# Applying two attention terms as two accumulated matmuls instead of one matmul of their sum

## The chip, the core and the metric

The kernel runs on one core of a Trainium2 chip. The core has TensorE (PE; its weight loads are listed as PEld), VectorE (DVE), ScalarE (ACT), GpSimd (POOL) and SyncE (SP), each with its own in-order queue, joined by semaphores. The metric is device microseconds of one execution.

## What is computed

A small language-model tower over x of shape (8, 1024): token embedding, a lattice attention with 8 heads, a causal attention and a mixture of experts. Only the lattice attention matters here. Per batch and head, on 1024x1024 scores:

```python
scores = ttt_filter(q @ k.T / 8)              # scaled by 1/PHI where int(|s|*1618) % 9 is 0, 3 or 6
attn = softmax(scores)
attn = attn * (sin(C1 * attn) * exp(-attn * attn / PHI) + cos(C2 * attn))
ctx = attn @ v
out = ctx @ Wo + bo
```

## The kernel before

The program runs four stages one behind the other: embed, lattice, causal, experts. The lattice stage handles 64 heads (8 batches of 8). For a head, att holds the softmax rows with queries on the partitions, as 8 row tiles of 128x1024. To apply them to the values, whose key index must be on the partitions, TensorE transposes them: `fill` (L565 to L574) turns four 128x128 blocks into one PSUM bank of 128x512. A head has 16 such half tiles, k (or d) = 0 to 15. TensorE turns each twice:

- gauss part (L607 to L614): half tile d to a bank, ScalarE squares it (L451) and takes the exponential (L463), VectorE multiplies with the bank into ag (L508).
- sine part (L615 to L625): half tile k again to one of four banks. ScalarE takes the cosine into work (L435), VectorE multiplies bank and work into work (L476): this is the cosine term. TensorE then subtracts whole turns in the bank (L586, a matmul with -I), ScalarE takes the sine in the bank (L440), VectorE multiplies bank and ag into sinb (L482): this is the sine term. GpSimd adds the two into sinb (L377, semaphore summed). TensorE multiplies the sum, in four 128x128 blocks, with the 128x64 values vo into outp (L635, semaphore av). I call these four matmuls an AV group; there are 16 a head, and all accumulate in the bank outp.

work and sinb are rings of 8 half tiles. outp is used in turn by the projections of the next head (L560), by the values (L646) and by the AV groups; VectorE adds the finished outp to the result at L487.

The order is written out by hand. Every engine runs the same loop over 44 steps a head and at each step does what the table of numbers at L283 to L297 places there, for three heads at once: the scores of head t (L599, then magnitudes on ScalarE L458 and the filter on VectorE), the exponentials and gauss part and early sine part of head t-1, the end of the sine part of head t-2. GAUSS is step 56 of a head, SINE step 72; fill k of the sine part is at SINE + k, its L586 at SINE + k + 3, L482 at SINE + k + 4, the GpSimd sum at SINE + k + 5, and AV group k at SINE + 6 + 8k/5 (L292). At one step TensorE takes first the oldest head's work. The exponentials (L423) start at step 47 of a head, that is step 3 of the 44; the first score matmul is at step 5 and stands behind a wait for the first exponential. In the loop body two heads are written out, so that every second head has the loop's branch in it, between steps 43 and 0, in the middle of the sine part's end.

GpSimd also scales six of the eight softmax rows (L382) and does one step of the filter (L387).

Of the kernel before, what the change touches and what calls it, by code (L numbers as in the profile page):

```python
# [6 lines left out]
ALU = mybir.AluOpType  # L7
# [6 lines left out]
P = 128  # L14
B, S, D = 8, 1024, 64
# [15 lines left out]
def wait(eng, s, v):  # L31

    if not isinstance(v, int) or v > 0:
        eng.wait_ge(s, v)
# [204 lines left out]
def lattice(nc, ident, hres, xT_dram, wvo, Wq, bq, Wk, bk):  # L239
# [4 lines left out]
    RING = 8  # L244
    with ExitStack() as ctx:
# [3 lines left out]
        def sem(name):  # L249
# [9 lines left out]
        vo = sb("vo", [P, TB, D])  # L259
# [15 lines left out]
        outp = ctx.enter_context(nc.psum_tensor("outp", [P, 512], F32))  # L275

        names = ("consts loadq loadv projd qk_sb vald v_sb qk mags rounded kept factor filtered bias expd "
                 "recip weights weights2 turned xpose squared gauss agd cosd acd nned sined tmul summed av outd").split()
        (consts, loadq, loadv, projd, qk_sb, vald, v_sb, qk, mags, rounded, kept, factor, filtered, bias,
         expd, recip, weights, weights2, turned, xpose, squared, gauss, agd, cosd, acd, nned, sined, tmul, summed,  # L280
         av, outd) = (sem("l_" + n) for n in names)

        NTILE = 2 * TB  # L283
# [5 lines left out]
        EXP = STEPS + 3  # L289
        GAUSS = STEPS + 12  # L290
        SINE = STEPS + 28
        AV = [SINE + 6 + 8 * k // 5 for k in range(NTILE)]  # L292
        OUT = AV[-1] + 1
        EV = 2
        PACE = 2
# [58 lines left out]
        @block.gpsimd  # L354
        def _(pool):
            nc.gpsimd.memset(xq[D:D + 1, :], 1.0).then_inc(consts, 1)
            pool.wait_ge(consts, 1)
            nc.gpsimd.memset(xv[D:D + 1, :], 1.0).then_inc(consts, 1)
            pool.wait_ge(consts, 2)
            nc.gpsimd.memset(negI[:], 0.0).then_inc(consts, 1)  # L360
            pool.wait_ge(consts, 3)
            nc.gpsimd.affine_select(out=negI[:], in_=negI[:], compare_op=ALU.not_equal, fill=-1.0,
                                    base=0, pattern=[[-1, P]], channel_multiplier=1).then_inc(consts, 1)
            nc.gpsimd.memset(halfpi[:], math.pi / 2).then_inc(consts, 1)
            pool.wait_ge(consts, 5)
            nc.gpsimd.memset(qT[D:P], 0.0).then_inc(consts, 1)
            pool.wait_ge(consts, 6)
            nc.gpsimd.memset(kT[D:P], 0.0).then_inc(consts, 1)

            def iteration(t, par):  # L370
                for s in range(STEPS):
                    for g, p, a in stages(t, par, s):
                        k = a - SINE - 5
                        if 0 <= k < NTILE:

                            wait(pool, tmul, NTILE * g + k + 1)
                            nc.gpsimd.tensor_tensor(sinb[:, k % RING], sinb[:, k % RING], work[:, k % RING],  # L377
                                                    ALU.add).then_inc(summed, 1)
                        j = a - EXP - 1
                        if 0 <= j < TB and j not in DVE_ROWS:  # L380
                            held(pool, recip, TB * g + j + 1)
                            nc.gpsimd.tensor_scalar(att[:, p, j], att[:, p, j], rs[:, j:j + 1], TURN,  # L382
                                                    ALU.mult, ALU.mult).then_inc(weights, 1)
                        if a - FACT in SCORE:
                            n = SCORE.index(a - FACT)
                            held(pool, kept, NTILE * g + n + 1)
                            nc.gpsimd.tensor_scalar(wgt[:, n % 4], wgt[:, n % 4], 1.0, PHI,  # L387
                                                    ALU.mult, ALU.add).then_inc(factor, 1)

            over_heads(pool, iteration)  # L390

        @block.scalar
        def _(act):
# [14 lines left out]
            def iteration(t, par):  # L408
                for s in range(STEPS):
                    for c in range(2):  # L410
                        if s == PROJ + EV + 2 * c and (not isinstance(t, int) or t + 1 < NHEADS):
                            projections(t + 1, 1 - par, c)
                    for g, p, a in stages(t, par, s):
                        if a == VAL + EV:

                            wait(act, vald, g + 1)
                            wait(act, av, NTILE * g)
                            nc.scalar.activation(vo[:], outp[:].rearrange("p (t d) -> p t d", d=D),
                                                 ACT.Copy, scale=1.0 / TURN).then_inc(v_sb, 1)
                        j = a - EXP  # L420
                        if 0 <= j < TB:
                            wait(act, bias, TB * g + j + 1)
                            nc.scalar.activation(att[:, p, j], att[:, p, j], ACT.Exp,  # L423
                                                 bias=nb[:, p, j:j + 1], scale=EXPSCALE,
                                                 accum_out=ssum[:, j:j + 1]).then_inc(expd, 1)
                        k = a - SINE - 1
                        if 0 <= k < NTILE:

                            wait(act, xpose, NX * g + NTILE + k + 1)

                            if k < RING:
                                wait(act, agd, NTILE * (g + 1) - RING + k + 1)
                            else:
                                wait(act, summed, NTILE * g + k - RING + 1)
                            nc.scalar.activation(work[:, k % RING], sine_bank(k), ACT.Sin,  # L435
                                                 bias=halfpi[:, 0:1], scale=-C2 / TURN).then_inc(cosd, 1)
                        k = a - SINE - 3
                        if 0 <= k < NTILE:
                            wait(act, nned, NTILE * g + k + 1)
                            nc.scalar.activation(sine_bank(k), sine_bank(k), ACT.Sin,  # L440
                                                 scale=2.0 * math.pi * (1.0 - 2.0 ** -22)).then_inc(sined, 1)

                    for g, p, a in stages(t, par, s):
                        d = a - GAUSS - 1
                        if 0 <= d < NTILE:
                            wait(act, xpose, NX * g + d + 1)
                            if d < RING:
                                wait(act, summed, NTILE * g - RING + d + 1)
                            else:
                                wait(act, agd, NTILE * g + d - RING + 1)  # L450
                            nc.scalar.activation(work[:, d % RING], gauss_bank(d), ACT.Square,  # L451
                                                 scale=1.0 / TURN).then_inc(squared, 1)
                    for g, p, a in stages(t, par, s):
                        if a - ABS in SCORE:
                            n = SCORE.index(a - ABS)
                            wait(act, qk, NTILE * g + n + 1)
                            wait(act, kept, NTILE * g + n - 3)
                            nc.scalar.activation(mag[:, n % 4], score_bank(n), ACT.Abs).then_inc(mags, 1)  # L458
                    for g, p, a in stages(t, par, s):
                        d = a - GAUSS - 1  # L460
                        if 0 <= d < NTILE:
                            wait(act, squared, NTILE * g + d + 1)
                            nc.scalar.activation(work[:, d % RING], work[:, d % RING], ACT.Exp,  # L463
                                                 scale=-1.0 / PHI).then_inc(gauss, 1)
# [84 lines left out]
        def _(pe):  # L549
# [26 lines left out]
            def iteration(t, par):  # L576
                for s in range(STEPS):
                    for g, p, a in stages(t, par, s):
# [47 lines left out]
                        if a in AV:  # L626
                            k = AV.index(a)

                            wait(pe, summed, NTILE * g + k + 1)
                            if k == 0:  # L630
                                wait(pe, v_sb, g + 1)
                            kt, half = k // 2, k % 2
                            for i in range(4):
                                o = (4 * half + i) * D
                                mm = nc.tensor.matmul(outp[:, o:o + D], sinb[:, k % RING, i * P:(i + 1) * P],  # L635
                                                      vo[:, kt, :], start=(k == 0 and i == 0),
                                                      stop=(k >= NTILE - 2), skip_group_check=True)
                            mm.then_inc(av, 1)
                        if a == VAL:
# [906 lines left out]
```

## Time and profile before

| | |
|---|---|
| time, median of 2 runs | 6786.28 us (6780.7 to 6791.86) |
| profiled execution, time | 6774.6 us |
| its span | 6772.9 us |
| mean granted TensorE clock, share of full | 0.892 |
| TensorE busy | 5442.1 us, 80% |
| TensorE weight loads busy | 3955.2 us, 58% |
| VectorE busy | 5082.3 us, 75% |
| ScalarE busy | 4262.2 us, 63% |
| GpSimd busy | 2754.5 us, 41% |
| L571, fills: idle before them, most of it until L508 | 873.6 us |
| L635, AV groups, busy | 1162.6 us |
| L377, GpSimd's sum, busy | 1289.3 us |

Busy time is the union of an engine's instructions. An f32 matmul shows as two records, so an AV group of 4 matmuls is 8 records. The ends of matmuls are modelled and reach beyond the start of the next one: the start of the next instruction tells better what a group costs. "Idle before" is the idle time of an engine directly ahead of an instruction, with what ended it. The granted clock is TensorE's, 1.00 for 2.4 GHz and 0.50 for 1.2 GHz.

### The profile page before, as it was taken

The numbers are of one execution on the slowest core, as the hardware profiler recorded it, in microseconds if no ns is written. First come the engines' busy times: TensorE is split into PE (matmuls) and PEld (weight loads), VectorE is DVE, ScalarE is ACT, GpSimd is POOL, SyncE is SP. The second block draws the span as 40 slices with busy tenths as digits, with TensorE's granted clock in tenths as the row PEclk, the third lists the DMA queues.
The fourth block names the chain that finished last, engine by engine and source line by source line (L and its number), as shares of the span: only waits on it lengthen the run. The fifth ranks groups of instructions, "written<-read, shape, count | busy, mean of one in ns | idle before, by whom it ended". The sixth has DMA issues, their size and how long they took to land. (4 is left out here: it accounts for less than half of the span.)

```text
span 6772.9 us, 115321 instructions
## 1 busy us (share of the span) xinstructions
PE 5442.1 (80%) x32426; PEld 3955.2 (58%) x32489; DVE 5082.3 (75%) x10177; ACT 4262.2 (63%) x7370; POOL 2754.5 (41%) x2639
## 2 busy tenths in 40 slices
PE   2788877787777877877888777778787799997999
PEld 1455555555555555555655555555555577775777
DVE  1888888888888888888888888888888555555443
ACT  1677777777777777777777777777777322222222
POOL 4445554444555544444555444445554200100111
PEclk9888898989889888888888889888988799898999
DMA  1000000000000000000000000000000000000000
GB/s 17 12 8 7 7 7 7 7 7 10 7 7 7 7 7 7 7 9 9 7 7 7 7 7 7 9 9 7 7 7 4 8 1 2 1 1 13 4 6 6
DMA packets 34500, 48.46 MB, mean 7 GB/s; under 512 B 24473, under 2 KB 24537, under 8 KB 34010
## 3 DMA queue, kind: packets, MB, share of 16 engines
q1 hardware_dynamic: 31962, 43.49, 2.5%
q14 instruction: 389, 3.19, 0.2%
q8 instruction: 101, 1.65, 0.1%
q0 software_dynamic: 2048, 0.14, 0.1%
HBM read 39.40 MB, written 4.19 MB: 6 GB/s over the span
## 5 line engine op out<-in xcount | busy, mean ns | idle before, releaser
L571 PE MATMUL banks<-ident,att 128*128 128x128 f32 x8192 | 1458.9, 311 | 873.6 <-DVE ag L508 496.8
L571 PEld LDWEIGHTS banks<-ident,att 128*128 128x128 f32 x8192 | 1024.2, 159 | 1568.6 <-DVE ag L508 1044.0
L377 POOL TENSOR_TENSOR sinb<-sinb,work 128x512 f32<-128x512 f32 x1024 | 1289.3, 1272 | 900.3 <-DVE sinb L482 898.3
L599 PE MATMUL banks<-kT,qT 128*128 128x512 f32 x2048 | 1262.5, 702 | 113.9 <-ACT att L423 104.0
L387 POOL TENSOR_SCALAR wgt<-wgt 128x512 f32<-128x512 f32 x1024 | 700.2, 684 | 1586.7 <-DVE wgt L502 1581.4
L635 PEld LDWEIGHTS outp<-vo,sinb 128*128 128x128 f32 x8192 | 1164.7, 216 | 214.9 <-issue 185.3
L635 PE MATMUL outp<-vo,sinb 128*128 128x64 f32 x8192 | 1162.6, 295 | 1.9 <-ACT att L423 1.9
L476 DVE TENSOR_TENSOR work<-banks,work 128x512 f32<-128x512 f32 x1024 | 699.8, 689 | 254.0 <-ACT work L435 183.6
L451 ACT ACTIVATE work<-banks 128x512 f32<-128x512 f32 x1024 | 609.9, 596 | 420.4 <-PE banks L571 411.6
L458 ACT ACTIVATE mag<-banks 128x512 f32<-128x512 f32 x1024 | 606.4, 594 | 356.2 <-PE banks L599 350.0
L435 ACT ACTIVATE work<-banks,halfpi 128x512 f32<-128x512 f32 x1024 | 695.4, 685 | 208.9 <-PE banks L571 139.6
L482 DVE TENSOR_TENSOR sinb<-banks,ag 128x512 f32<-128x512 f32 x1024 | 694.9, 686 | 114.6 <-ACT banks L440 111.6
L508 DVE TENSOR_TENSOR ag<-banks,work 128x512 f32<-128x512 f32 x1024 | 699.5, 683 | 77.3 <-ACT work L463 77.3
L502 DVE SCALAR_TENSOR_TENSOR wgt<-wgt,mag 128x512 f32<-128x512 f32 x1024 | 716.0, 699 | 0.0
L440 ACT ACTIVATE banks<-banks 128x512 f32<-128x512 f32 x1024 | 593.5, 585 | 176.6 <-PE banks L586 175.1
L463 ACT ACTIVATE work<-work 128x512 f32<-128x512 f32 x1024 | 640.4, 625 | 8.5
L497 DVE TENSOR_SCALAR wgt<-mag 128x512 f32<-128x512 f32 x1024 | 529.8, 517 | 140.1 <-ACT mag L458 133.7
L423 ACT ACTIVATE att<-att,nb 128x1024 f32<-128x1024 f32 x512 | 581.2, 1137 | 0.8
L382 POOL TENSOR_SCALAR att<-att,rs 128x1024 f32<-128x1024 f32 x384 | 530.1, 1381 | 110.1 <-DVE rs L492 82.2
L870 ACT ACTIVATE c_pr<-c_sc,c_nm 128x128 f32<-128x128 f32 (+7 forms) x256 | 189.5, 740 | 585.4 <-DVE c_nm L935 569.4
L599 PEld LDWEIGHTS banks<-kT,qT 128*128 128x128 f32 x2048 | 346.2, 211 | 252.8 <-DVE mx L535 118.8
L586 PE MATMUL banks<-negI,nturn 128*128 128x128 bf16 x4096 | 424.8, 232 | 71.8 <-DVE work L476 68.7
(194 smaller groups left out, 6740.6 us busy)
## 6 DMA issues: line engine op xcount, KB each, us to landing
xq<-xT_dram SPq DMA_DIRECT2D x64, 256.0 KB
xv<-xT_dram SPq DMA_DIRECT2D x64, 256.0 KB, 3.7
xT_dram<-xT SPq DMA_DIRECT2D x8, 256.0 KB, 2.9
out<-hres SPq DMA_DIRECT2D x8, 256.0 KB, 2.6
base<-in_L_tok_turns,idx POOLq DMA_INDIRECT x64
wqk<-in_L_attn_Wq SPq DMA_DIRECT2D x64, 16.0 KB
wqk<-in_L_attn_Wk SPq DMA_DIRECT2D x64, 16.0 KB
wqk<-in_L_attn_bq SPq DMA_DIRECT2D x64, 0.2 KB
```

The source lines that it names most:

```text
L377: nc.gpsimd.tensor_tensor(sinb[:, k % RING], sinb[:, k % RING], work[:, k % RING], ALU.add).then_inc(summed, 1)
L387: nc.gpsimd.tensor_scalar(wgt[:, n % 4], wgt[:, n % 4], 1.0, PHI, ALU.mult, ALU.add).then_inc(factor, 1)
L435: nc.scalar.activation(work[:, k % RING], sine_bank(k), ACT.Sin, bias=halfpi[:, 0:1], scale=-C2 / TURN).then_inc(cosd, 1)
L451: nc.scalar.activation(work[:, d % RING], gauss_bank(d), ACT.Square, scale=1.0 / TURN).then_inc(squared, 1)
L463: nc.scalar.activation(work[:, d % RING], work[:, d % RING], ACT.Exp, scale=-1.0 / PHI).then_inc(gauss, 1)
L476: nc.vector.tensor_tensor(work[:, k % RING], sine_bank(k), work[:, k % RING], ALU.mult).then_inc(acd, 1)
L482: nc.vector.tensor_tensor(sinb[:, k % RING], sine_bank(k), ag[:, k], ALU.mult).then_inc(tmul, 1)
L502: nc.vector.scalar_tensor_tensor(wgt[:, n % 4], wgt[:, n % 4], ROUND, mag[:, n % 4], ALU.subtract, ALU.is_gt).then_inc(kept, 1)
L508: nc.vector.tensor_tensor(ag[:, d], gauss_bank(d), work[:, d % RING], ALU.mult).then_inc(agd, 1)
L571: mm = nc.tensor.matmul(bank[:, i * P:(i + 1) * P], att[:, p, 4 * half + i, kt * P:(kt + 1) * P], ident[:], is_transpose=True, start=(i == ...
L599: nc.tensor.matmul(score_bank(n), qT[:, p, (n // 2) * P:(n // 2 + 1) * P], kT[:, p, (n % 2) * 512:(n % 2 + 1) * 512], start=True, stop=Tru ...
L635: mm = nc.tensor.matmul(outp[:, o:o + D], sinb[:, k % RING, i * P:(i + 1) * P], vo[:, kt, :], start=(k == 0 and i == 0), stop=(k >= NTILE ...
```

## The change

GpSimd's sum is dropped, with its semaphore. AV group k now consists of 8 matmuls: for each of the four 128x128 blocks one with the cosine term in work as the stationary operand and one with the sine term in sinb, both accumulated into the same columns of outp. It waits for the two products themselves (acd and tmul). The groups stand one a step, at SINE + 6 + k. ScalarE's waits for a free place in work now are for the AV group instead of for the sum.

```diff
@@ -289,7 +289,7 @@
-        AV = [SINE + 6 + 8 * k // 5 for k in range(NTILE)]
+        AV = [SINE + 6 + k for k in range(NTILE)]
@@ -370,12 +370,6 @@
-                        k = a - SINE - 5
-                        if 0 <= k < NTILE:
-
-                            wait(pool, tmul, NTILE * g + k + 1)
-                            nc.gpsimd.tensor_tensor(sinb[:, k % RING], sinb[:, k % RING], work[:, k % RING],
-                                                    ALU.add).then_inc(summed, 1)
@@ -431,7 +425,7 @@
                             if k < RING:
                                 wait(act, agd, NTILE * (g + 1) - RING + k + 1)
                             else:
-                                wait(act, summed, NTILE * g + k - RING + 1)
+                                wait(act, av, NTILE * g + k - RING + 1)
@@ -445,7 +439,7 @@
                             if d < RING:
-                                wait(act, summed, NTILE * g - RING + d + 1)
+                                wait(act, av, NTILE * g - RING + d + 1)
@@ -626,14 +620,18 @@
                         if a in AV:
                             k = AV.index(a)
 
-                            wait(pe, summed, NTILE * g + k + 1)
+                            wait(pe, acd, NTILE * g + k + 1)
+                            wait(pe, tmul, NTILE * g + k + 1)
                             if k == 0:
                                 wait(pe, v_sb, g + 1)
                             kt, half = k // 2, k % 2
                             for i in range(4):
                                 o = (4 * half + i) * D
+                                nc.tensor.matmul(outp[:, o:o + D], work[:, k % RING, i * P:(i + 1) * P],
+                                                 vo[:, kt, :], start=(k == 0 and i == 0),
+                                                 stop=False, skip_group_check=True)
                                 mm = nc.tensor.matmul(outp[:, o:o + D], sinb[:, k % RING, i * P:(i + 1) * P],
-                                                      vo[:, kt, :], start=(k == 0 and i == 0),
+                                                      vo[:, kt, :], start=False,
                                                       stop=(k >= NTILE - 2), skip_group_check=True)
                             mm.then_inc(av, 1)
```

First place, TensorE in the sine part, before: fills (L571), turn subtractions (L586) and AV groups (L635), four matmuls a row.

```order
L571 MATMUL banks<-ident,att 128x128 x4
L635 MATMUL outp<-vo,sinb 128x64 x4
L586 MATMUL banks<-negI,nturn 128x128 x4
L571 MATMUL banks<-ident,att 128x128 x4
L586 MATMUL banks<-negI,nturn 128x128 x4
L571 MATMUL banks<-ident,att 128x128 x4
L635 MATMUL outp<-vo,sinb 128x64 x4
```

The same place now; fills are L565, turn subtractions L580, the two matmuls of an AV group L630 and L633.

```order
L565 MATMUL banks<-ident,att 128x128 x4
L630 MATMUL outp<-vo,work 128x64
L633 MATMUL outp<-vo,sinb 128x64
L630 MATMUL outp<-vo,work 128x64
L633 MATMUL outp<-vo,sinb 128x64
L630 MATMUL outp<-vo,work 128x64
L633 MATMUL outp<-vo,sinb 128x64
L630 MATMUL outp<-vo,work 128x64
L633 MATMUL outp<-vo,sinb 128x64
L580 MATMUL banks<-negI,nturn 128x128 x4
L565 MATMUL banks<-ident,att 128x128 x4
```

Between two fills there now is always an AV group, and it has eight matmuls.

Second place, TensorE from the last turn subtraction of a head (L586) to the first score matmuls (L599) of a later one, before. L34 rows are register and semaphore work.

```order
L586 MATMUL banks<-negI,nturn 128x128 x4
L34 REGISTER_ALU
L635 MATMUL outp<-vo,sinb 128x64 x4
L34 REGISTER_ALU
L635 MATMUL outp<-vo,sinb 128x64 x4
L34 REGISTER_ALU
L34 ISA x2
L599 MATMUL banks<-kT,qT 128x512
L34 REGISTER_ALU
L635 MATMUL outp<-vo,sinb 128x64 x4
L34 REGISTER_ALU x2
L635 MATMUL outp<-vo,sinb 128x64 x4
```

Now, the end of that place: the last L580 stands 32 matmuls, four AV groups, ahead of the first score matmul (L593).

```order
L630 MATMUL outp<-vo,work 128x64
L633 MATMUL outp<-vo,sinb 128x64
L34 REGISTER_ALU
L34 ISA x2
L593 MATMUL banks<-kT,qT 128x512
L34 REGISTER_ALU x3
L593 MATMUL banks<-kT,qT 128x512
L34 REGISTER_ALU x3
L593 MATMUL banks<-kT,qT 128x512
```

Before, two AV groups stood ahead of the first score matmul and six behind it; now four stand ahead of it and none behind.

## Rows read from the trace of the kernel before

**Rows 1.** The page's first line.

```profile
span 6772.9 us, 115321 instructions
```

**Rows 2.** Windows view: busy us (x instructions) of each engine, granted clock, DMA.

```profile
2000.00:3000.00 1000.00, 788.58 (x4716) 570.20 (x4714) 837.82 (x1723) 757.57 (x1290) 496.13 (x477) 0.89 0.03 8
```

**Rows 3.** Timeline of TensorE: start, us, line, [idle before <-releaser]; L646 once a head.

```profile
2081.75 2.00 PE L646 MATMUL outp<-wvo,xv 65*128 x16
2159.60 1.67 PE L646 MATMUL outp<-wvo,xv 65*128 x14
```

**Rows 4.** Lines view of 2000 to 2800 us: busy, mean ns, idle before.

```profile
L377 POOL TENSOR_TENSOR sinb<-sinb,work 128x512 f32<-128x512 f32 x160 | 201.5, 1272 | 137.1 <-DVE sinb L482 136.7
L635 PE MATMUL outp<-vo,sinb 128*128 128x64 f32 x1280 | 178.5, 291 | 0.0
```

**Rows 5.** Timeline of TensorE, end of one sine part and the first scores.

```profile
2095.00 0.66 PE L571 MATMUL banks<-ident,att 128*128 128x128 f32 x4 [0.63 <-DVE sinb L482]
2095.49 1.00 PE L635 MATMUL outp<-vo,sinb 128*128 128x64 f32 x8
2096.33 0.39 PE L586 MATMUL banks<-negI,nturn 128*128 128x128 bf16 x4
2096.55 0.61 PE L571 MATMUL banks<-ident,att 128*128 128x128 f32 x4
...
2109.01 0.61 PE L571 MATMUL banks<-ident,att 128*128 128x128 f32 x4
2109.45 1.00 PE L635 MATMUL outp<-vo,sinb 128*128 128x64 f32 x8
2110.29 0.61 PE L586 MATMUL banks<-negI,nturn 128*128 128x128 bf16 x8
...
2111.63 0.39 PE L586 MATMUL banks<-negI,nturn 128*128 128x128 bf16 x4
...
2115.32 1.12 PE L599 MATMUL banks<-kT,qT 128*128 128x512 f32 x2 [1.51 <-ACT att L423]
2116.28 1.89 PE L635 MATMUL outp<-vo,sinb 128*128 128x64 f32 x16
2118.01 1.08 PE L599 MATMUL banks<-kT,qT 128*128 128x512 f32 x2
```

**Rows 6.** Lines L476 and L482, 2000 to 2800 us: ns min/median/max.

```profile
L476 DVE TENSOR_TENSOR work<-banks,work x160: 680/691/693, 2009.3 to 2747.9; 128x512 f32<-128x512 f32 x160
L482 DVE TENSOR_TENSOR sinb<-banks,ag x160: 680/686/693, 2011.5 to 2750.1; 128x512 f32<-128x512 f32 x160
```

**Rows 7.** Timeline of ScalarE in the same head.

```profile
2110.72 1.07 ACT L440 ACTIVATE banks<-banks 128x512 f32<-128x512 f32 x2 [0.33 <-PE banks L586]
...
2118.49 0.57 ACT L458 ACTIVATE mag<-banks 128x512 f32<-128x512 f32 x1
```

**Rows 8.** Timeline of VectorE in the same head.

```profile
2111.33 2.03 DVE L482 TENSOR_TENSOR sinb<-banks,ag 128x512 f32<-128x512 f32 x3 [0.22 <-ACT banks L440]
...
2119.19 0.56 DVE L497 TENSOR_SCALAR wgt<-mag 128x512 f32<-128x512 f32 x1 [1.54 <-ACT mag L458]
```

**Rows 9.** Timeline of TensorE, the last AV groups of the last head.

```profile
5280.52 7.31 PE L635 MATMUL outp<-vo,sinb 128*128 128x64 f32 x64
```

**Rows 10.** Timeline of TensorE, a head with the branch.

```profile
2015.48 1.00 PE L635 MATMUL outp<-vo,sinb 128*128 128x64 f32 x8
...
2033.29 0.40 PE L586 MATMUL banks<-negI,nturn 128*128 128x128 bf16 x4 [0.38 <-DVE work L476]
```

**Rows 11.** Timeline of VectorE at that branch.

```profile
2030.87 0.69 DVE L476 TENSOR_TENSOR work<-banks,work 128x512 f32<-128x512 f32 x1 [2.33 <-issue]
```

**Rows 12.** Timeline of TensorE, two AV groups of a later head.

```profile
2348.92 2.94 PE L635 MATMUL outp<-vo,sinb 128*128 128x64 f32 x16
```

**Rows 13.** Windows view: stretch with scores, and start of the gauss part.

```profile
2115.30:2124.80 9.50, 8.36 (x49) 6.18 (x49) 6.02 (x16) 9.50 (x18) 6.65 (x7) 1.00 0.00 0
...
2130.20:2134.30 4.10, 4.10 (x19) 3.35 (x20) 4.10 (x10) 1.71 (x3) 0.86 (x2) 0.62 0.00 0
```

More of the change, by code:

```diff
@@ L277, in lattice @@
         names = ("consts loadq loadv projd qk_sb vald v_sb qk mags rounded kept factor filtered bias expd "
-                 "recip weights weights2 turned xpose squared gauss agd cosd acd nned sined tmul summed av outd").split()
+                 "recip weights weights2 turned xpose squared gauss agd cosd acd nned sined tmul av outd").split()
         (consts, loadq, loadv, projd, qk_sb, vald, v_sb, qk, mags, rounded, kept, factor, filtered, bias,
-         expd, recip, weights, weights2, turned, xpose, squared, gauss, agd, cosd, acd, nned, sined, tmul, summed,
+         expd, recip, weights, weights2, turned, xpose, squared, gauss, agd, cosd, acd, nned, sined, tmul,
          av, outd) = (sem("l_" + n) for n in names)
```

## The prediction

> **What bounds the kernel now.** I read the page's header first, then the windows view in stretches of 1,000 us, to see where the time is. The span is 6772.9 us [rows 1]. A stretch in the middle shows TensorE at 788.58 of 1000 us and VectorE at 837.80 [rows 2]. Neither is full. That is the attention part. The starts of two L646 groups, one group per head, stand 77.85 us apart [rows 3], and 1,280 records of L635 in 800 us at 128 a head make it 80.0 us a head on average [rows 4]. 64 heads of 80 us are 5,120 us, so three quarters of the program is a repetition of one head, and a microsecond per head is 64 us.
>
> A share of 79% says nothing of which engine ends a stage, so I went to the timeline of one head. A head has three parts. In the gauss part L571 waits for VectorE's L508. In the sine part every step k is, on TensorE, one fill (L571), one group of L586, and now and then one group of L635. TensorE there still waits 0.6 us at about every second fill for VectorE's L482 [rows 5]: it has room, but little. From the fill at 2095.00 to the one at 2109.01 there are 9 steps in 14.01 us, 1.56 us a step. VectorE's two operations per step take 0.69 us each [rows 6], 1.38 us of the 1.56: it sets this pace. Behind the sine part ScalarE sets the pace: table load, exponentials, first magnitudes, without a pause [rows 7]. TensorE puts score matmuls and the left-over groups of L635 between them. Then TensorE waits until VectorE and GpSimd have scaled the rows.
>
> So TensorE's idle time is real but spread: mainly at the wait before the gauss part and in the gauss part, with only some 0.3 us a step in the sine part.
>
> **What the change removes.** GpSimd's sum, 1,272 ns, 16 a head [rows 4], and with it one hand-over between L482 and the AV group. Nobody on the path waits for it: the AV groups are placed so late that they start as soon as the engine is free [rows 5]. VectorE's L482 takes 680 to 693 ns at least and at most, whatever GpSimd does beside it [rows 6], so a quiet GpSimd can give VectorE at most 13 ns on 32 operations, 0.4 us a head. I take 0. GpSimd is also free earlier for the first att scaling, but what reads that next, VectorE's nturn, stands behind the first operation on a magnitude at 2119.19 [rows 8], so I take 0 here too. The two waits of ScalarE that go from the sum to av ask for AV group k-8, which stands three steps ahead in TensorE's order: 0.
>
> **What it adds.** Each AV group becomes 8 matmuls instead of 4. A single group takes 0.84 us from its start to the next instruction (2095.49 to 2096.33), two together 1.73 (2116.28 to 2118.01) [rows 5], and a run of eight in the last head 7.31 us, 0.16 of them the tail, so 0.89 each [rows 9]. The new group has the instruction count of two old ones, with other data: 1.73 us. Over 16 groups that is 14.2 us more TensorE work a head.
>
> On this price there are rules. The row shows that a 128x64 matmul with its own 128x128 block costs 105 ns a record (0.84 us over 8). The Trainium skill, "TensorE: Matmul & The Clock Gate", section "LDWEIGHTS (loading the stationary operand)", says a weight load takes its columns over 1.2 GHz, 107 ns for 128, so the block and not the 64 moving columns is paid for; the trace agrees. Its section "Back-to-back issue gap" gives isolated matmuls of up to 64 columns only about 60 cycles (25 ns), by which the 8 added records would cost 0.2 us a group, an estimate, and the change would vanish in the waits.
>
> **What it moves.** AV group k now stands at sine step k+6 instead of 6+8k/5. Before, seven groups stood beside the fills of steps 6 to 15. Now each of these ten steps has one. Step by step:
>
> 1. A step of TensorE in the sine part: fill 0.44 to 0.49 us, L586 0.22, AV 1.73 [rows 5], together 2.42 us against 1.56 now. It passes VectorE's 1.38 by far: TensorE becomes the bound there. The loop through L586, ScalarE's sine, VectorE's product and the next fill is some 2.1 us by the same rows (L586 at 2110.29 [rows 5], sine at 2110.72 [rows 7], product at 2111.33 to 2112.0 [rows 8], plus hand-overs) and is just hidden.
> 2. From the first AV group to the last L586 of the head TensorE must issue 12 AV groups, 9 fills and 11 groups of L586: 12 x 1.73 + 9 x 0.47 + 11 x 0.22 = 27.4 us. Now it is 2095.49 to 2111.63, 16.1 us, and in a head with the loop's branch in it 2015.48 to 2033.29, 17.8 us [rows 5, 10]. In the latter VectorE stands 2.3 us at the branch with no releaser [rows 11]; behind a late TensorE that is hidden. The loss is 11.3 and 9.6 us, 10.4 on average.
> 3. Behind the last L586 stand now four AV groups, 4 x 1.78 = 7.1 us, and only then the first score matmul, 7.4 us after that L586 started instead of 3.7 (2111.63 to 2115.32) [rows 5]. ScalarE wants that score 6.9 us after it (2118.49) [rows 7]. The score is ready some 0.9 us after its start, the start-to-start of a score being 0.96. So ScalarE's first magnitude comes at 8.3 instead of 6.9, and the remaining exponentials with it: 1.4 us. VectorE is idle before 2119.19 waiting for this very result [rows 8], so nothing absorbs it.
> 4. Given back: AV groups between the scores and the one in the gauss part go away. Where the granted clock falls to half, these cost double: a pair at 2348.92 took 2.94 us instead of 1.95 [rows 12], ahead of a score on which ScalarE waits. I saw it in two of three heads with the branch and in none of three others at this place. I take 0.4 us a head on average, between 0 and 1.
>
> Sum: 10.4 + 1.4 - 0.4 = 11.4 us a head, times 64 = 730 us. On the profiled execution's 6774.6 us (its span is 6772.9) this gives 7505 us; that run lies 0.2% below the median shown, 6786.28, which would put it at 7516. I say **7510**.
>
> Bounds: at the low end the groups cost 0.84 x 2 (2 is then 9.8 us), the score is hidden, and the give-back is 1 us: 8.8 us a head, 7340. At the high end the loop of step 1 adds 0.1 us a step over 12 steps, nothing is given back and a first score at half clock (0.96 more) delays ScalarE: 10.4 + 1.2 + 1.4 + 1.0 = 14.0, plus a little more of the next paragraph, 7700.
>
> **Rivals.**
> *The clock in the thin stretch (slower still).* The granted clock is 1.00 in the stretch with scores and AV groups between them, TensorE busy 8.36 of 9.50 us. After the wait that follows it is 0.62, between its levels 1.2 and 2.4 GHz, for 4.1 us [rows 13]. Without the six groups there the stretch is busy for only some 4 of 9.5 us, so the clock may fall earlier and stay at half further into the gauss part, where a step of TensorE (fill 0.45 and score 0.96) grows from 1.4 to 2.8 us against the some 2.2 us at which VectorE lets it go. Four such steps are 2.4 us a head: 7510 + 154 = 7664. The Trainium skill, "TensorE: Matmul & The Clock Gate", section "HAM oscillation — how this bites in real kernels", warns of exactly such idle gaps that re-throttle the clock at each round; the trace agrees for the wait before the gauss part. The chance I give this case is 9%.
>
> *It fits in the idle time (no change).* TensorE is busy 63.1 us of an 80 us head; 14.2 us more makes 77.3, still under 80: 6780. For it speaks only the average. Against it the order: engines run their queues in order, ten of the groups stand between fills for which ScalarE and VectorE wait, and the room there is 0.3 us a step. A middle course, the added records at a fraction of the row's price, gives up to +9 us a head, 6780 to 7350: 8% in all, 3% of it within 2%.
>
> *GpSimd's sum was the brake (faster).* If what now paces a sine step were the sum's hand-over, a step could fall from 1.56 to VectorE's 1.38 us: 0.18 x 16 = 2.8 us a head, 180 us, 6595. It decides only if TensorE's step stays under 1.38, that is if the doubled group costs less than 0.69 us, under today's 0.84 for half of it. 2%.
>
> **How the numbers follow.** TensorE-bound sine part as worked out, 81%; clock 9%; partly or wholly hidden 8%; faster 2%. 2% of the time is about what a measurement of this kernel can tell from no change. Slower by over 2% is 0.81 + 0.09 + 0.05 = 0.95, within it 0.03, faster 0.02. The range 7340 to 7700 holds the first two cases and leaves out the rest.
>
> **What would show it.** Step 1: in the sine part L571 no longer waits for L482, fills stand 2.4 us apart, VectorE and ScalarE wait for TensorE, granted clock 1.00. Step 2: 27 us from the first AV group to the last L586 in both kinds of head. Step 3: four groups in a row, then a score, and ScalarE's first magnitude waits for it by 1.4 us. Step 4: no AV group between scores. Wrong would be fills under 2.0 us apart (cheaper matmuls), a half clock inside the dense stretch (then much more than 7700), or a gauss part that is longer or shorter than today's.

## The result and the profile after

The changed kernel takes 7851.26 us (7834.71 to 7867.8, 2 runs) against 6786.28 us: ratio 1.1577, 95% interval 1.1529 to 1.1626. The direction was forecast, the size was not: 7510 us with a range to 7700.

The page of the changed kernel: span, busy times, TensorE's instruction queue (q8: packets, MB, share), and the costliest groups (busy, mean ns | idle before).

```profile
span 7832.9 us, 130950 instructions
PE 6532.1 (83%) x40681; PEld 5006.3 (64%) x40681; DVE 5063.3 (65%) x10177; ACT 4254.7 (54%) x7370; POOL 1479.3 (19%) x1615
q8 instruction: 399, 6.54, 0.4%
L633 PE MATMUL outp<-vo,sinb 128*128 128x64 f32 x8192 | 1729.4, 296 | 0.0
L630 PE MATMUL outp<-vo,work 128*128 128x64 f32 x8192 | 1694.2, 292 | 0.0
L476 DVE TENSOR_TENSOR sinb<-banks,ag 128x512 f32<-128x512 f32 x1024 | 705.9, 689 | 926.3 <-ACT banks L434 923.8
```

The same queue on the page before:

```profile
q8 instruction: 101, 1.65, 0.1%
```

VectorE's second product, now L476, waits 926 us for ScalarE's sine (115 us before), which stands behind the late TensorE. The busy times of L630 and L633 can't be added, since a record of the one runs on while the next of the other starts. The windows view of the AV groups alone (tile vo, the whole span) has both lines together:

```profile
0.00:7833.00 7833.00, 2172.59 (x16384) 2135.38 (x16384) 38.27 (x64) 0.87 0.03 7
```

2173 us are 1.87 times the 1162.6 of before, for twice the records.

Windows view of the changed kernel, against [rows 2]: TensorE 47 us per 1000 busier, VectorE 155 less.

```profile
2000.00:3000.00 1000.00, 835.75 (x5247) 652.00 (x5247) 682.64 (x1409) 614.64 (x1050) 194.24 (x220) 0.86 0.03 7
```

A sine step of the changed kernel in TensorE's timeline: fill, the AV group (first and last pair of records), turn subtraction, next fill.

```profile
2000.20 0.61 PE L565 MATMUL banks<-ident,att 128*128 128x128 f32 x4
2000.65 0.33 PE L630 MATMUL outp<-vo,work 128*128 128x64 f32 x2
...
2002.16 0.39 PE L633 MATMUL outp<-vo,sinb 128*128 128x64 f32 x2
2002.38 0.39 PE L580 MATMUL banks<-negI,nturn 128*128 128x128 bf16 x4
2002.60 0.61 PE L565 MATMUL banks<-ident,att 128*128 128x128 f32 x4
```

2.40 us a step, 1.73 for the group, no wait for VectorE: as forecast. But at the loop's branch, between AV groups 9 and 10 of every second head, TensorE's timeline has this, for which [rows 10] have nothing of TensorE's own:

```profile
2202.22 0.39 PE L633 MATMUL outp<-vo,sinb 128*128 128x64 f32 x2
2204.26 0.40 PE L580 MATMUL banks<-negI,nturn 128*128 128x128 bf16 x4 [1.66 <-issue]
...
2205.97 0.63 PE L630 MATMUL outp<-vo,work 128*128 128x64 f32 x2
2206.39 0.64 PE L633 MATMUL outp<-vo,sinb 128*128 128x64 f32 x2
```

TensorE starts nothing for 2.0 us (1.66 of them idle by the records), and behind it a pair of records takes 0.43 us instead of 0.22. The windows view of that head (ahead of the branch, behind it) and of the next head's whole dense stretch, from its first AV group to its first score; the third number from the end is the granted clock:

```profile
2179.20:2202.30 23.10, 23.10 (x232) 23.10 (x231) 11.72 (x20) 10.68 (x18) 0.00 (x0) 1.00 0.01 3
2204.90:2225.50 20.60, 20.60 (x102) 20.60 (x103) 3.04 (x6) 7.49 (x12) 2.24 (x2) 0.50 0.00 0
2282.30:2316.90 34.60, 34.60 (x341) 34.60 (x341) 15.27 (x25) 18.95 (x31) 2.24 (x2) 1.00 0.01 2
```

After 2.0 us without a matmul the clock fell to 1.2 GHz and stayed there for 20.6 us in which TensorE was busy without a gap. It was still at 1.2 GHz at the first score matmuls; over all fallen heads it rose 2.0 to 5.3 us behind the first of them. The next head, without a branch, runs the same work at 2.4 GHz.

The traces grouped by head say how often. For each of heads 2 to 59 I took the time from the first AV group to the last turn subtraction (column 1), from there to the first score (2) and to the first magnitude on ScalarE (3), and from sine part to sine part (4), in us, as means. "Fell" counts heads with half clock for at least three tenths of the time of the AV groups between the last subtraction and the score.

| kernel, heads | fell | 1 | 2 | 3 | 4 |
|---|---|---|---|---|---|
| before, no branch | 0 of 29 | 16.16 | 3.69 | 6.86 | 78.43 |
| before, branch | 11 of 29 | 17.87 | 3.83 | 6.91 | 80.96 |
| after, no branch | 0 of 29 | 27.35 | 7.37 | 8.56 | 91.27 |
| after, branch, not fallen | 3 of 29 heads | 29.22 | 7.37 | 8.56 | 93.44 |
| after, branch, fallen | 26 of 29 heads | 32.31 | 14.08 | 16.22 | 103.64 |

A head without a branch is 12.8 us longer, one with a branch 21.6 (102.58 on average against 80.96). That is 17.2 a head, and with the ends, where less is lost, the 1060 us between the two spans.

### The profile page after: what moved, and what is told of

The parts are those of the page before. It is cut to its first block and busy times, and to the rows that moved or that the text cites. A ratio compares the mean times of both kernels' runs of the same rounds, so it can differ in the third digit from the quotient of the medians.

```text
span 7832.9 us, 130950 instructions
## 1 busy us (share of the span) xinstructions
PE 6532.1 (83%) x40681; PEld 5006.3 (64%) x40681; DVE 5063.3 (65%) x10177; ACT 4254.7 (54%) x7370; POOL 1479.3 (19%) x1615
## 3 DMA queue, kind: packets, MB, share of 16 engines
q0 software_dynamic: 2048, 0.14, 0.1%
## 5 line engine op out<-in xcount | busy, mean ns | idle before, releaser
L565 PE MATMUL banks<-ident,att 128*128 128x128 f32 x8192 | 1493.1, 318 | 790.3 <-DVE ag L502 463.3
L565 PEld LDWEIGHTS banks<-ident,att 128*128 128x128 f32 x8192 | 1069.5, 163 | 1593.1 <-DVE ag L502 1023.3
L633 PE MATMUL outp<-vo,sinb 128*128 128x64 f32 x8192 | 1729.4, 296 | 0.0
L630 PE MATMUL outp<-vo,work 128*128 128x64 f32 x8192 | 1694.2, 292 | 0.0
L593 PE MATMUL banks<-kT,qT 128*128 128x512 f32 x2048 | 1296.4, 725 | 160.2 <-ACT att L417 150.9
L633 PEld LDWEIGHTS outp<-vo,sinb 128*128 128x128 f32 x8192 | 1386.1, 212 | 0.0
L630 PEld LDWEIGHTS outp<-vo,work 128*128 128x128 f32 x8192 | 1383.6, 212 | 0.2
L476 DVE TENSOR_TENSOR sinb<-banks,ag 128x512 f32<-128x512 f32 x1024 | 705.9, 689 | 926.3 <-ACT banks L434 923.8
L593 PEld LDWEIGHTS banks<-kT,qT 128*128 128x128 f32 x2048 | 369.5, 221 | 450.5 <-issue 161.3
L580 PE MATMUL banks<-negI,nturn 128*128 128x128 bf16 x4096 | 441.9, 236 | 86.8 <-issue 43.1
```

What stands on the lines that cost most here:

```text
L476: nc.vector.tensor_tensor(sinb[:, k % RING], sine_bank(k), ag[:, k], ALU.mult).then_inc(tmul, 1)
L565: mm = nc.tensor.matmul(bank[:, i * P:(i + 1) * P], att[:, p, 4 * half + i, kt * P:(kt + 1) * P], ident[:], is_transpose=True, start=(i == ...
L593: nc.tensor.matmul(score_bank(n), qT[:, p, (n // 2) * P:(n // 2 + 1) * P], kT[:, p, (n % 2) * 512:(n % 2 + 1) * 512], start=True, stop=Tru ...
L630: nc.tensor.matmul(outp[:, o:o + D], work[:, k % RING, i * P:(i + 1) * P], vo[:, kt, :], start=(k == 0 and i == 0), stop=False, skip_group ...
```

## The experiments

Theory A: the doubled groups cost what was worked out; the rest is the branch, by TensorE's stall there and the clock that falls in it.

**e1, e2: fewer branches.** The changed kernel with 4, then 12 heads in the loop body (12 shown).

```diff
-            with eng.Fori(1, NHEADS // 2 - 1) as i:
-                iteration(2 * i, 0)
-                iteration(2 * i + 1, 1)
+            with eng.Fori(0, (NHEADS - 4) // 12) as i:
+                for j in range(12):
+                    iteration(12 * i + (2 + j), j % 2)
```

> The changed kernel with four heads written out in the loop body instead of two: 15 branches instead of 30, nothing else. Theory A (TensorE stalls some 1.9 us at the branch in the middle of the AV groups, the granted clock falls to 1.2 GHz there and stays until the first score: a head with the branch is 102.6 us against 91.3 us): 15 times 11.3 us less, 170 us, so 7680 us. Rival B (the clock falls because of the long dense stretch itself, or with some period of its own, and the branch only coincides): the falls stay, only 15 stalls of 1.9 us go: 7820 us. In the trace A wants half clock in branch heads only, one in four.

> The changed kernel with twelve heads in the loop body, 5 branches instead of 30. Theory A: 25 times 11.3 us less, 283 us: 7570 us, which is near the 7510 us of the prediction. Rival B: 25 stalls of 1.9 us less, 7800 us. A third possibility is that straight code of this length stalls on instruction loads in other places, then it lies between.

Measured 7672.1 us (ratio to before 1.1301, 1.1257 to 1.1345) and 7585.82 us (1.1177, 1.1135 to 1.1218). By head: the clock fell in 14 of 14 and 4 of 4 heads with a branch and in none of the 44 and 54 others, which take 91.5 and 91.6 us. The loss goes with the branches; rival B, by which the dense stretch itself brings the clock down, is out.

**e3: the kernel before with 12 heads in the body.** The same edit.

> The kernel before with twelve heads in the loop body. Its branch heads last 80.9 us against 78.4 us. Theory A: the branch costs it only that, so 25 times 2.5 us less, 63 us: 6723 us, 0.93% faster. Rival B expects the same or 0.

Measured 6728.38 us, ratio 0.9919 (0.9888 to 0.9949): faster than both kernels, by 0.8% against 0.9% expected.

**e4: the move alone.** `AV = [SINE + 6 + k ...]` in the kernel before.

> The kernel before, with GpSimd's sum and single AV groups of four matmuls, but the groups placed at SINE + 6 + k as in the changed kernel: only the move, without the doubled work. Theory A and the prediction's steps: a step of TensorE is 0.47 + 0.22 + 0.84 = 1.53 us, no more than the 1.56 us of today, so within 1% of 6786 us; 12 groups, 9 fills and 11 turn subtractions make 16.7 us from the first AV group to the last subtraction against 16.2 us, at worst 0.5 us a head, 32 us. Rival C (it is the placing of the groups ahead of the scores that costs, by the order, not by the work): 3 us or more a head, over 6980 us.

Measured 6802.31 us, ratio 1.0026 (1.0009 to 1.0044). Rival C, by which the placing costs and not the work, is out. Heads without a branch take 78.94 us, 0.5 more. In the branch heads the clock falls in 24 of 29, though TensorE's longest idle time there is only 0.4 to 0.8 us, but the single groups cost half as much, and the head is only 0.5 us longer than before.

**e5, e6, e15: empty instructions.** e5 and e6 put 72 `pe.nop` at steps 0 and 36 into e2, e15 put 480 into TensorE's loop body of the kernel before.

> Twelve heads in the loop body, as e2 (7586 us), and at step 0 of every second head, where the branch used to be, 72 empty instructions of about 50 ns in TensorE's queue, enough to drain what it has queued ahead and leave it idle for about 2 us. Theory A (an idle time of about 2 us at this place is enough to bring the clock down, and the stretch of AV groups that follows doesn't bring it up): about 27 more heads with stall and half clock, 11 to 12 us each, 300 to 330 us more: 7900 us. Rival E (it is something else in the branch, as its instruction loads, and not the idle time): only the pause itself, 27 x 2 us: 7640 us.

> The same pause in every second head, but at step 36, where fills and turn subtractions stand between the AV groups for 8 more steps. Theory A (it takes the idle time and a stretch of AV groups alone behind it): the clock falls seldom or comes back before the AV groups stand alone, 2 to 7 us a pause, 7650 to 7800 us. Rival D (an idle time of 2 us decides alone, and AV groups hold the clock down also when fills stand between them): seven sine steps of 2.4 us and the groups behind at half clock, 20 us or more a pause: over 8200 us.

> The kernel before with 480 empty instructions in TensorE's loop body, in steps 14 to 23, where it waits for VectorE at each step; they left no idle time in e5 and e6. Its body grows from 1691 recorded instructions to about 2170 with them. Theory H: TensorE's branch takes 3.3 us or more instead of 0.2, its instruction queue loads packets through the whole run, branch heads have a stall of TensorE of about 2 us and fall to half clock more often than 11 in 29; VectorE and ScalarE stall there by themselves for 2.3 us already, so the time grows by only 0 to 2 us per branch, 6780 to 6850 us. Rival I: branch 0.2 us, trace as before.

Measured 7568.75, 7581.72 and 6781.69 us, as the kernels they were made from. The built programs turned out to hold none of these empty instructions, so the runs say nothing on the theories; they are repeats of e2 and of the kernel before.

**e9, e10: a real wait without a branch.** e2, with TensorE waiting for two GpSimd memsets in every second head. GpSimd's part, then TensorE's (e9, with cuts; e10 has 80 in place of 88, which is step 36, and waits for AV group 1 in place of 9):

```diff
+                        if a == 88 and p == 0:
+                            held(pool, av, NTILE * g + 10)
+                            if 3 > 1:
+                                nc.gpsimd.memset(pad[:, 0:1024], 0.0).then_inc(padded, 2)
+                                held(pool, padded, g + 2)
+                            nc.gpsimd.memset(pad[:, 0:512], 0.0).then_inc(paused, 2)
...
+                        if a == 88 and p == 0:
+                            wait(pe, paused, g + 2)
+                            pe.nop(nofuse=True)
```

> Twelve heads in the body, as e2 (7586 us). The empty instructions of e5 and e6 left no idle time in the trace, so here TensorE waits: at step 0 of every second head, for two GpSimd memsets that start when AV group 9 is done, some 1.5 us of work and hand-overs, so TensorE is idle for about 2 us where the branch used to be. Theory A (idle time here brings the clock down and the AV groups behind don't bring it up): 27 more heads with stall and half clock, 11 to 12 us each: 7890 us, half clock in nearly all heads with the wait and in none without. Rival E (something else in the branch does it): 27 times 2 us, 7640 us, no falls.

> The same wait at step 36 of every second head, behind AV group 1, with fills and turn subtractions between the AV groups for 8 more steps. Theory A1 (AV groups with fills between them bring the clock back): 2 us of idle time and up to 5 of half clock a head, under 7800 us. Rival D (once down, the clock stays down through all of the sine part): over 20 us a head, 8150 us or more.

e9 measured 7919.47 us, ratio 1.1656 (1.1633 to 1.1679), as theory A has it. TensorE's timeline at the wait of a head that has no branch, and the windows view behind it:

```profile
2832.15 0.59 PE L590 MATMUL banks<-negI,nturn 128*128 128x128 bf16 x4 [1.98 <-POOL pad L379]
```

```profile
2832.40:2852.80 20.40, 20.40 (x104) 20.40 (x101) 2.40 (x5) 7.67 (x12) 2.24 (x2) 0.50 0.01 2
```

The clock fell in 29 of 29 heads with the wait (104.2 us a head) and in none of the 29 without (91.1). Four of the 29 also have one of the five branches; the other 25 haven't. Idle time of 1.98 us is enough at this place; the branch isn't needed.

e10 measured 8154.01 us, ratio 1.1989 (1.1957 to 1.2020). Theory A1, by which groups with fills between them bring the clock back, was wrong, and rival D right. In 20 of 29 heads the clock fell at the wait and stayed down through the rest of the sine part, fills included (120.2 us a head). In one more it fell only at the loop's branch (106.7 us), and in 8 not at all (93.8). The windows view of a fallen head, ahead of the wait and behind it:

```profile
2511.60:2515.60 4.00, 4.00 (x41) 4.00 (x40) 2.85 (x5) 2.02 (x4) 0.00 (x0) 1.00 0.00 0
2518.30:2576.00 57.70, 57.70 (x296) 57.70 (x295) 13.47 (x21) 17.84 (x28) 2.24 (x2) 0.50 0.00 1
```

57.7 us at half clock, every one of them busy; in the next head the 34.6 us from first AV group to first score ran at full clock. The Trainium skill, "TensorE: Matmul & The Clock Gate", "Part 1: The HAM clock gate", describes the gate as opened by sustained matmul work; the trace doesn't agree for this mix of AV groups, fills and turn subtractions. The clock stayed up through it in one head and wasn't raised by it in the other.

**e7: the doubled groups at the old places.**

> The changed kernel with the groups at SINE + 6 + 8k/5 as before: doubled groups, no sum, but the old places. First AV group to last subtraction is then 8 groups, 9 fills, 11 subtractions, 20.5 us instead of 27.4; two groups, 3.5 us, ahead of the first score; the others between scores where ScalarE sets the pace and hides about half of them. Theory A: 4 us a head in the sine part, 2 to 3 behind it, and in branch heads the stall and some half-clock groups, 4 to 6 more: about 9.5 us a head, 7400 us. Rival F (the added work costs its 14 to 17 us a head wherever it stands): 7800 us.

Measured 8156.82 us, ratio 1.2030 (1.2005 to 1.2055): slower than the changed kernel, against the 7400 us that I expected and also above rival F's 7800. The waits view of 2000 to 3000 us shows what I had left out, total us, times, longest:

```profile
ACT work L429 <- PE outp L633: 141.0, 39, 5.4
PE banks L565 <- DVE sinb L476: 57.5, 68, 1.9
```

ScalarE now waits for a place in work, which only the late AV group frees, and TensorE's next fill in turn waits for VectorE. TensorE's longest idle time is 1.7 to 1.9 us in each head without the branch and up to 3.5 us in those with it, and the clock fell in 58 of 58: 100.6 us a head. So the move to one group a step belongs to the change: with work freed by the AV group and no longer by the sum, the old places cost 306 us more.

**e8: the doubled matmuls taken away.** The matmul on `work` in the AV group is gone and its `start` stands at the one on sinb, so the cosine term is missing from the result.

> The changed kernel with the matmuls on work left out, so that only the sine term is applied and the cosine term is missing from the result; no sum by GpSimd, groups of four matmuls, one a step. It shows what the move and the missing sum do without the doubled matmuls. Theory A: like e4, 6780 to 6810 us, the missing sum gives nothing. Rival G (the sum held something up or slowed VectorE): under 6720 us.

Measured 6764.19 us, ratio 0.9982 (0.9965 to 0.9999). Rival G, by which the sum held something up, is out. By the ratios e8 is 0.4% under e4, all of it in the branch heads (80.0 us against 81.5; the others take 79.0 and 78.9). In e4 the clock fell in 24 of them, here in 1. That one head tells most. It is the only one in this run whose branch record is long, 3.95 us against 0.21 to 0.25 in the others that are taken, and TensorE's timeline behind it has:

```profile
600.61 0.60 PE L580 MATMUL banks<-negI,nturn 128*128 128x128 bf16 x4 [2.96 <-issue]
```

The clock then was at half for 13.7 us, and the head took 86.8 us: stall and fall together, in a kernel whose other branch heads have neither at this place.

**e12, e13: the branch moved within the loop.** The order of instructions is unchanged, the loop is cut elsewhere; e12 does so for TensorE in the changed kernel (first = 11), e13 for all four engines in the kernel before.

```diff
+            def chunk(t, par):
+                iteration(t, par, range(first, STEPS))
+                if not isinstance(t, int) or t + 1 < NHEADS + 2:
+                    iteration(t + 1, 1 - par, range(first))
...
+            with eng.Fori(1, NHEADS // 2 - 1) as i:
+                chunk(2 * i, 0)
+                chunk(2 * i + 1, 1)
```

> The changed kernel with two heads in the loop body as it was, 30 branches, but TensorE's loop cut at step 11 instead of 0: the order of its instructions is the same, only the branch stands where TensorE waits some 4 us ahead of the gauss part anyway. Theory A: no stall in the AV groups, no fall of the clock behind them: 30 times 11.3 us less, 7510 us, all heads at 91 us. Rival E (a branch costs its time wherever it stands, or the clock falls for another reason): 7800 us or more.

> The kernel before with each engine's loop cut where that engine waits: TensorE at step 11, ScalarE at 13, VectorE at 4, GpSimd at 28. Its branch heads take 2.5 us longer than the others, so 30 x 2.5 = 75 us less, 6705 us, 1.1% faster than before, if the branch is hidden on all four; 0 if one of them still shows it.

e12 measured 7544.41 us, ratio 1.1116 (1.1094 to 1.1137): 307 us less than the changed kernel with as many branches, and within 0.5% of the forecast of 7510. No head fell, all take 27.36, 7.37 and 8.56 us in columns 1 to 3, and the granted clock of 2000 to 3000 us is 0.91 instead of 0.86. TensorE's branch record still lasts 3.3 to 3.9 us there: the stall isn't gone, it stands where TensorE waits anyway.

e13 measured 6733.5 us, ratio 0.9924 (0.9906 to 0.9941), the same as e3, 0.8% instead of the 1.1% expected.

**e14, e16: why the branch stalls TensorE.** The branch's own record lasts 0.08 to 0.25 us in the kernel before and 3.3 to 4.0 us in the changed one (0.08 the last time, when it isn't taken), and between 1000 and 5000 us TensorE's instruction queue loads nothing in the first and 206 packets in the second. The loop body grew from 1691 recorded instructions to 2228. e14 makes it shorter, with part of the cosine term missing from the result, and leaves the groups at the branch doubled:

```diff
-                                nc.tensor.matmul(outp[:, o:o + D], work[:, k % RING, i * P:(i + 1) * P],
-                                                 vo[:, kt, :], start=(k == 0 and i == 0),
-                                                 stop=False, skip_group_check=True)
+                                if k >= 8:
+                                    nc.tensor.matmul(outp[:, o:o + D], work[:, k % RING, i * P:(i + 1) * P],
+                                                     vo[:, kt, :], start=False,
+                                                     stop=False, skip_group_check=True)
                                 mm = nc.tensor.matmul(outp[:, o:o + D], sinb[:, k % RING, i * P:(i + 1) * P],
-                                                      vo[:, kt, :], start=False,
+                                                      vo[:, kt, :], start=(k == 0 and i == 0),
```

> The changed kernel without the cosine matmuls of AV groups 0 to 7, so that part of the cosine term is missing from the result. These groups stand ahead of the branch; the groups at and behind it are doubled as before. TensorE's loop body shrinks from 2228 recorded instructions to about 1972. Without branch effects a head is 8 x 0.84 us shorter than 91.3: 84.5 us. Theory H (the stall is TensorE's reload of its own instructions at the branch, which sets in when its body no longer fits, somewhere between the 1716 instructions of e8, with a branch of 0.2 us, and the 2228 of the changed kernel, with one of 3.3 to 4.0 us): if the body fits again, branch 0.2 us, no instruction packets in the middle of the run, no fall of the clock in the AV groups, 7110 us. Rival I (a branch with doubled AV groups behind it costs this whatever the body's size, or the limit is under 1972): falls in most branch heads, 7420 us.

Measured 7463.51 us, ratio 1.1013 (1.0975 to 1.1051): as rival I, branch record 3.7 to 4.5 us, 29 of 29 branch heads fallen, the other heads at 84.6 us as expected. So 1972 instructions are still too many, but 1687 in e13 also have the long branch and 1691 before have not: the size alone isn't it. e16 moves the old body:

```diff
+            for _ in range(256):
+                pe.wait_ge(consts, 7)
+
             project(0, 0)
```

> The kernel before with 256 waits on a semaphore that is long there, ahead of TensorE's first projection. They become 128 instructions of about 50 ns, 6 us once. The loop body keeps its 1691 recorded instructions, only its place in the instruction stream moves by 128. In the program files TensorE's body with its branch lies in 7 blocks of 256 instructions in each of the kernels whose branch record was 0.2 us (before, e4, e8), and in 8 or more in each with one over 3 us (after, e1, e2, e3, e7, e12, e13, e14); with the shift it lies in 8. Theory J (the number of blocks that the body touches decides whether TensorE reloads it): branch record over 3 us, about 220 packets in TensorE's instruction queue between 1000 and 5000 us where before had none, TensorE idle for about 2 us at the branch; time 0 to 2 us more per branch since VectorE and ScalarE stand still there anyway: 6780 to 6850 us. Rival K (the amount of instructions or the doubled groups decide): branch 0.2 us, no packets, 6785 us.

Measured 6850.02 us, ratio 1.0108 (1.0091 to 1.0125), at the upper end of the 6780 to 6850 expected, with the body unchanged. Branch record 3.3 to 3.9 us, 224 packets where there were none, the clock fell in 25 of 29 branch heads instead of 11. Its page has:

```profile
q8 instruction: 364, 5.96, 0.4%
```

Theory J holds: the place of the body counts. In the built programs it touches 7 blocks of 256 instructions in the three kernels with the short branch (before, e4, and e8 but for one time in 30), 8 in e13 and e16, and 9 or more in the others, which all have the long one. The Trainium skill, "Runtime: NRT & Kernel Launch", section "Instruction fetch mechanics", gives TensorE a store of 2048 instructions refilled in blocks of 256, and a fetch before the engine can go on where a taken branch's target isn't in the current window of two blocks. The runs agree with the stall and fit the block as the unit, but don't agree with a window of two blocks on TensorE: a body over 7 blocks looped without a reload, and the limit lies between 7 and 8.

## Why the prediction was right and wrong

*What bounds it, and the price of a group: right.* A group of eight matmuls takes 1.73 us, a sine step 2.40 (2.42 forecast), and TensorE is the bound there. *Step 2, heads without a branch: right.* 27.35 us against 27.4. *Step 3: right.* The first score comes 7.37 us behind the last subtraction (7.4), the first magnitude 8.56 (8.3), 1.7 later than before instead of 1.4. In the changed kernel's timeline of ScalarE the forecast wait stands, 1.6 us instead of 1.4:

```profile
2318.14 0.60 ACT L452 ACTIVATE mag<-banks 128x512 f32<-128x512 f32 x1 [1.61 <-PE banks L593]
```

*Step 4: too large.* The rest of a head without a branch, column 4 less 1 and 3, is 55.36 us against 55.41: nothing is given back. These small misses together are 12.8 us a head instead of 11.4 to 12.3 for such heads, and e12, which has only them, takes 7544 us.

*Step 2, heads with the branch: this is the step that failed.* I wrote that VectorE stands 2.3 us at the branch and "behind a late TensorE that is hidden". TensorE's own branch isn't in the sum at all: I put it at nothing without a reason, for a body that the change makes a third longer. It cost nothing before because the old body touched 7 blocks (e16). The changed one touches 10, so TensorE reloads it at each of the 29 branches that are taken, and it was now the bound at just this place: 1.9 us idle in each branch head, and 29.2 us instead of 27.4 in step 2 even where the clock held. In most of them the clock fell in that time, and the AV groups left before the first score ran at half of it: 10.2 us more in a fallen head than in one that hadn't fallen. Together 11.3 us a branch. Of the 341 us between the forecast of 7510 and the 7851 measured, e12 puts 307 on the branch and leaves 34 for the small misses; e1 and e2 take their share by the number of branches.

*The rival on the clock: right on the kind, wrong on the place.* I looked for the fall in the thin stretch behind the groups. Nothing was lost there (the 55.36 us above). I did write that half clock inside the dense stretch would give much more than 7700 us, but gave it no chance, since the dense stretch had no wait in it by the sum. *It fits in the idle time:* out, by the sine step of 2.40 us. *The sum was the brake:* out, by e8, whose heads without a branch are no faster than those of e4.

What isn't settled is what decides in the single head. In the changed kernel TensorE starts nothing for 1.8 to 2.6 us (2.2 on average) in the 26 branch heads that fell and for 1.9 us in the 3 that didn't; in e10, with 2.3 us in each, the wait brought the clock down in 20 of 29. And stalls of 2 us aren't the only way: the branch heads of e4 and e8 have about the same longest idle times, 0.4 to 0.8 and 0.4 to 0.7 us, yet in e4 the clock fell in 24 and in e8 in none but the one with the long branch. Nor is it shown what VectorE and ScalarE wait for at the branch: their branch records last 0.04 to 0.06 us in every run, and they stand 2.3 and 2.1 us behind it in the kernel before.

## What to carry to other kernels

When a change adds instructions to a loop, look at the loop's branch on each engine: the length of its record, and the packets of that engine's instruction queue in the middle of the run. If the body is reloaded, the branch costs about 2 us on TensorE, and it costs the whole path if the engine is the bound where the branch stands. The remedy is free: cut the loop where that engine waits anyway, or write out more iterations (here 307 and 265 us on the changed kernel, 0.8% on the old one either way).

Doubling a bound engine's work in one stage is priced by that stage's own order, not by its average idle time; and an idle time of 2 us in a dense stretch like this one may cost ten more, by the clock.

## What the runs showed that I had not expected

- 57.7 us of gapless TensorE work at 1.2 GHz (e10), against 34.6 us of the same kind of work at 2.4 GHz in the next head: what ran before, not what runs, set the level. In the changed kernel, e9 and e10 the rise came 2.0 to 5.3 us behind the first score matmul, never in the AV groups.
- TensorE starting nothing for 1.8 to 2.6 us brought the clock down in 26 of 29 heads (after), and for 2.3 us in 29 of 29 (e9).
- Moving an unchanged loop body by 128 instructions made the kernel before 1.1% slower (e16).
